# Soft attention kinds: GpSimd adds up the four whole key blocks, and one product with ones replaces four

## What is computed

```
x = x + attn_a(layernorm(x))   # "squared": scores squared instead of a softmax
x = x + ffn(layernorm(x))      # "gated": one key and value shared by the heads, picked by a top-1 gate; softmax
x = x + attn_b(layernorm(x))   # "mqa": one key and value shared by the heads; softmax; output projection
x = x + ffn(layernorm(x))      # "gated" again

# a soft kind, for one head:
att = softmax(where(causal, q @ k.T / sqrt(32), -inf))   # exp(scores - row maximum) / (sum of exp)
y   = att @ v
```

## Time and profile before

| | us |
|---|---|
| median of three runs | 4967.37 (4939.61 to 4968.83) |
| the profiled execution | 4950.15, of which the span 4948.4 |
| TensorE busy in the span | 4254.0 (86%) |
| VectorE busy | 1771.8 (36%) |
| ScalarE busy | 1551.4 (31%) |
| GpSimd busy | 850.5 (17%) |

### The profile page before, as it was taken

The page is one execution under the profiler, slowest core; times in us unless marked ns, Lnnn a source line. Parts: engine busy times, 40 slices in busy tenths (PEclk is TensorE's granted clock), DMA queues, the critical chain, the costliest instruction groups (busy, mean ns, idle before and its releaser), DMA issues.

```text
span 4948.4 us, 76270 instructions
## 1 busy us (share of the span) xinstructions
PE 4254.0 (86%) x32674; PEld 1835.6 (37%) x32674; DVE 1771.8 (36%) x2666; ACT 1551.4 (31%) x1985; POOL 850.5 (17%) x1495
## 2 busy tenths in 40 slices
PE   7899999969797887887888888888898987978886
PEld 4444434324333333333333333333333333333332
DVE  1222222224334433344343343433434344333342
ACT  1443343421323223233333333332223233232333
POOL 1212121110102102012021111212012012020011
PEclk9999999989999898999989999999999998999999
DMA  1001010030001001001010010101001001010010
GB/s 60 18 17 36 9 43 5 31 95 8 15 1 39 14 1 52 1 3 50 1 52 1 20 33 7 46 1 52 1 1 52 1 18 35 1 52 1 1 35 27
DMA packets 63404, 115.65 MB, mean 23 GB/s; under 512 B 8672, under 2 KB 9184, under 8 KB 63072
## 3 DMA queue, kind: packets, MB, share of 16 engines
q1 hardware_dynamic: 63072, 110.77, 6.9%
HBM read 77.19 MB, written 33.55 MB: 22 GB/s over the span
## 4 chain that ended last, share of the span: by engine, by line
PE 60%; DVE 6%; ACT 4%; issue 4%; POOL 2%; DMA 2%; SPq 0%; POOLq 0%; DVEq 0%
PE banks L1030 16%; PE banks L989 11%; PE banks L943 9%; PE banks L973 8%; PE banks L937 7%; DVE maxima_soft L771 5%; ACT probs_soft L692 4%; PE banks L970 3%; PE banks L998 2%; PE banks L1127 2%; DMA tiles_soft<-out 1%; POOL rest_soft L665 1%; POOL tiles_soft L597 1%; PE banks L1039 0%; PE banks L949 0%
## 5 line engine op out<-in xcount | busy, mean ns | idle before, releaser
L771 DVE TENSOR_REDUCE maxima_soft<-banks 128x2 f32<-128x1024 f32 (+3 forms) x1152 | 1036.5, 952 | 1507.3 <-PE banks L998 924.8
L692 ACT ACTIVATE probs_soft<-banks 128x1024 f32<-128x1024 f32 (+1 forms) x960 | 848.5, 936 | 1286.4 <-PE banks L973 1286.3
L989 PE MATMUL banks<-k_soft,q_soft 32*128 32x512 f32 (+3 forms) x4608 | 585.1, 578 | 215.9 <-ACT probs_soft L692 215.7
L606 POOL TENSOR_SCALAR_AFFINE_SELECT probs_soft<-probs_soft 128x512 f32<-128x512 f32 x384 | 239.2, 635 | 1841.5 <-ACT probs_soft L692 1839.2
L973 PE MATMUL banks<-q_soft,k_soft 32*128 32x512 f32 (+3 forms) x4608 | 487.2, 504 | 0.0
L1030 PE MATMUL banks<-probs_soft,v_soft 128*32 128x512 f32 (+3 forms) x4608 | 423.7, 510 | 2.0 <-POOL probs_soft L606 2.0
L1030 PE MATMUL banks<-probs_soft,ones 128*32 128x512 f32 (+3 forms) x4608 | 401.4, 489 | 0.0
L970 PE MATMUL banks<-shift_soft,ones 32*128 32x512 bf16 (+3 forms) x2304 | 201.2, 336 | 218.3 <-DVE maxima_soft L771 195.4
L989 PEld LDWEIGHTS banks<-k_soft,q_soft 32*128 32x128 f32 x4608 | 197.2, 194 | 463.5 <-issue 449.3
L692 ACT ACTIVATE probs_squared<-banks 128x1024 f32<-128x1024 f32 (+1 forms) x320 | 282.8, 936 | 239.8 <-PE banks L973 239.5
L1030 PEld LDWEIGHTS banks<-probs_soft,v_soft 128*32 128x32 f32 x4608 | 137.7, 113 | 278.6 <-issue 253.7
(11 more groups left out here) (151 smaller groups left out, 4206.8 us busy)
## 6 DMA issues: line engine op xcount, KB each, us to landing
tiles_soft<-out SPq DMA_DIRECT2D x96, 256.0 KB, 2.8
rest_soft<-out SPq DMA_DIRECT2D x96, 256.0 KB, 3.2
out<-rest_soft SPq DMA_DIRECT2D x96, 256.0 KB, 2.0
tiles_squared<-in_x SPq DMA_DIRECT2D x32, 256.0 KB, 2.9
rest_squared<-in_x SPq DMA_DIRECT2D x32, 256.0 KB, 3.2
out<-rest_squared SPq DMA_DIRECT2D x32, 256.0 KB, 2.0
raw_wq<-in_squared_wq SPq DMA_DIRECT2D x1, 1024.0 KB, 6.0
raw_wk<-in_squared_wk SPq DMA_DIRECT2D x1, 1024.0 KB, 8.2
```

The lines of the kernel that those rows point to most:

```text
L606: ins = pool.affine_select(out=cells, in_=cells, compare_op=ALU.is_ge, fill=0.0, base=0, pattern=[[0, HG], [1, P]], channel_multiplier=-1)
L692: act.activation(slot(ph, n)[:, 2 * a:2 * a + 2, 0:width], score_pair(e, a)[:, :, 0:width], ACT.Exp if soft else ACT.Square, scale=SCALE). ...
L771: ins = dve.reduce_max(m["maxima"][:, ph % 2, 2 * a:2 * a + 2, t, p], score_pair(e, a)[:, :, col:col + P * blocks], AX_X)
L989: ins = pe.matmul(psum[:, score_bank(e, i), col:col + P * blocks], m["q"][D * i:D * i + D, ph % NG, P * t:P * t + P], k_of(ph)[D * i:D * i ...
```

## The change

In soft kinds GpSimd adds the four slots of part B to one tensor full_sum (128 x 4 x 512 float32) in three instructions: at burst 4 slot 3 plus slot 4, at burst 5 that plus slot 5, at burst 6 that plus slot 6. Each waits for both exps of its burst and for the add before it. sm B then is 4 products with full_sum in place of 16, and waits for the third add. sm B moves from half 16 to half 17 in both acts, so behind rows(8) and mxr in the second. To make room in SBUF, logit_parts and v_parts become one buffer, side_parts. Weights of the planner stay.

```diff
+FULL = [n for n, burst in enumerate(KEY_BURSTS) if burst[1] == "B"]
...
         at[h].append(("av", of, part))
-        at[h + 1].append(("sm", of, part))
+        at[h + 2 if part == "B" else h + 1].append(("sm", of, part))
...
+        m["full_sum"] = sb("full_sum", [P, HG, CHUNK])
-        m["logit_parts"] = sb("logit_parts", [P, NC, CHUNK])
-        m["v_parts"] = sb("v_parts", [P, NC, CHUNK])
+        m["logit_parts"] = m["v_parts"] = sb("side_parts", [P, NC, CHUNK])
...
+                    elif soft and n > FULL[0]:
+                        pool.wait_ge(sg.probs_ready, 2 * (of_kind[e] + 1))
+                        added = (len(FULL) - 1) * ph + n - FULL[0] - 1
+                        if n == FULL[1] and ph:
+                            wait_work(pool, ("sm", ph - 1, part))
+                        elif n > FULL[1]:
+                            pool.wait_ge(sg.probs_added, added)
+                        before = slot(ph, FULL[0])[:] if n == FULL[1] else m["full_sum"][:]
+                        pool.tensor_tensor(m["full_sum"][:], before, slot(ph, n)[:], ALU.add).then_inc(sg.probs_added, 1)
...
+                    if u == "sm" and soft and part == "B":
+                        pe.wait_ge(sg.probs_added, (len(FULL) - 1) * (ph + 1))
+                        for i in range(HG):
+                            ins = pe.matmul(out[D * i:D * i + D, :], k["ones"][:], m["full_sum"][:, i, :], start=True, stop=True)
+                        products = []
```

More of the change, by code:

```diff
@@ L258, in __init__ @@
         self.probs_masked = sem("probs_masked")
+        self.probs_added = sem("probs_added")
         self.rows_scored = sem("rows_scored")
```

## The result

The changed kernel takes 4809.2 us in the median (4795.75 to 4812.38, 4 runs) against 4953.49 us before: ratio 0.9705, 95% interval 0.9658 to 0.9753. 88 us less were forecast, 144 came. The profiled execution took 4811.47 us with a span of 4809.8, against 4950.15 and 4948.4 before: 138.6 us less of span.

A forecast was written before the change was run, and what follows sets the result against it. The prediction took TensorE's list of work, with short holes, as the bound. Removal and holes gave 120.0 us; minus 14 (stage starts) and 18 (clock) left 88 us gained, so 4870 us was predicted, range 4830 to 4925.

The forecast's parts named there:

- What is removed, 131.0 us: TensorE at sm B: 3 of 4 product sets go, 2.73 us in each of 48 phases, 131.0 us saved.
- The holes, 25.2 + 7.4 us opened and 28.2 us closed: Around rows(8): moving sm B opens waits in front, 25.2 and 7.4 us, and fills those before keys(9), 28.2 us won.
- One assumption under it: In the 16 phases with fillers, the planner was expected to put the filler in front of rows(8); 6.2 us lost.
- The adds: On GpSimd: 144 adds of 4.47 us, 643 us more, beside other work, costing nothing below 8.7 us an add.
- The stage starts, 14 us: Phases 4, 8, 36 and 40: residual adds behind the third add end 3.5 us later, delaying loads; 14 us lost.
- the statement that in the other stages the stats stand far behind the adds: Other stages: outs and stats stand 11 us of PE work or more behind the add, or loads come behind burst 9.
- The clock, -18 us: Second act: the thin stretch grows, so the clock falls once more in one of four phases, 12 x 1.5 = 18 us lost.
- My bounds for it (0 to 73 us lost): Extra clock falls: from no more often (0) to once more in each of the 48 phases (73 us).
- In the first act nothing.: First act: the order of bursts and sm B doesn't change and its products stay, so no time change.
- The rival that had nothing lost: Clock falls as often as before and four stage starts absorb the delay: 120 to 131 us gained, 4830 to 4840; chance 0.13.

The follow-up runs named there:

- e9: Changed kernel with each GpSimd add one burst later, but sm B's 16 products from the slots kept and the adds' result unused; ratio 0.986 to the kernel before.
- e1: Kernel before with sm B, all 16 products, moved from half 16 to half 17, no adds; the planner rearranged other work; 4873.0 us, ratio 0.9863.
- e3: Changed kernel with sm B's 16 products from the slots kept, adds made and waited for but their result unused; 4900.95 us, ratio 0.9922 to the kernel before.
- e0: The changed kernel itself, measured again beside later runs on the same chip; 4808.23 us, ratio 0.9728 to the kernel before.
- e5: Changed kernel with each GpSimd add one burst later in GpSimd's order; 4787.83 us, ratio 0.9688 to the kernel before.
- e2: Changed kernel with sm B left at half 16, in front of rows(8), adds and 4 products kept; ratio 0.988 to the kernel before.
- e8: Kernel before with 4 products in place of 16, sm B at half 16, no adds, sum leaving out three blocks; ratio 0.985.
- e12: Kernel before, sm B still 16 products at half 16, plus four sets of idle products (16 products) behind rows(8); ratio 1.0214.
- e13: Kernel before with 4 products at half 16, no adds, three blocks left out, plus one idle set behind rows(8); ratio 0.9809.
- e11: Changed kernel with adds one burst later, plus 216 idle sets of 4 products of 384 columns between adjoining keys and rows bursts; 4745.18 us, ratio 0.9585.

## Why the prediction was right or wrong

It was wrong: the time, 4809.2 us, lies below the range of 4830 to 4925, and the gain is 1.6 times the forecast. The step that failed is the clock, which was to cost 18 us and gave a gain. Step by step:

- **What is removed, 131.0 us: nearly.** The group of products with ones went from 277.0 to 102.3 us, and the new line has 51.1 us: 123.6 us. A set that stands alone takes 1.07 us with its tail, not 0.91.
- **The holes, 25.2 + 7.4 us opened and 28.2 us closed: right.** PE's wait for exp grew by 35.3 us (215.7 to 251.0), that for maxima shrank by 22.0 (195.4 to 173.4; forecast 28.2 - 6.2 = 22.0). One assumption under it held only in part: of the 16 phases with fillers the filler went in front of rows(8) in 10; in phases 16, 20, 24, 28, 30 and 34 the planner left no filler beside rows(8) at all. That both sums come out so near is partly luck.
- **The adds: right in size and in place.** 4.51 us against 4.47, and PE waited for an add in one of 48 phases, 1.8 us. e9 shows that 144 of them beside this TensorE work cost nothing that could be measured (0.986, against 0.9863 in e1 without adds). What they would have cost on VectorE no run shows. VectorE's 576 large reductions took 1.221 us each, before 1.220: nothing.
- **The stage starts, 14 us: right for the four phases, but two more were hit.** e1 to e3, where only the adds differ, shows 14.1 us more of waiting in phases 4, 8, 36 and 40. Phases 21 and 25 add 8.9 us: the statement that in the other stages the stats stand far behind the adds went by the old plan, and the move changed the plan. The adds ahead of outputs and stats cost 20 (e0 to e5) to 28 us (e1 to e3), of which 17 and 24 are these waits. What else there is may be the clock (401 us at half clock in e0, 363 in e5), but that isn't shown. Against the kernel before the waits grew by only 9 us (135.4 to 144.2), since the move shortened them: 117.3 in e1. ln(0) in phase 4 waited 3.35 us longer, 3.5 forecast, but all such waits of that phase together stayed at 11 us.
- **The clock, -18 us: the step that failed, in its sign.** The rows showed a thin stretch (PE busy 7.11 of 12.8 us at 1.00) ahead of one at 0.51, and I reckoned the stretch by its length only: it got longer, so the clock had to get worse. My bounds for it (0 to 73 us lost) left no room for a gain. It got better, from 487 to 406 us at half clock, which by the estimate above is worth up to half of 81 us; the matmuls that stayed took 32.8 us less. e1 shows that this comes with the move and not by chance (0.962 to 0.966 against 0.948 to 0.954); e2 and e8 show that the change without the move would have gone as I feared and worse (0.988 and 0.985). I had treated the move as a matter of two holes, 28.2 - 32.6 us, that is a loss of 4; measured alone it is a gain of 68 us. How much of it is sm B's new place and how much the other work that the planner moved with it stays open; e12 and e13, which leave that work alone, show that dense work in the new place raises the clock by itself (0.961 to 0.962 against 0.950 to 0.954, and 0.951 to 0.954 against 0.932 to 0.944 in e8).
- **"In the first act nothing."** It was 9.5 us shorter in the profiled execution (GpSimd's first instruction of the second act at 1086.86, before at 1096.37). Most of it is the spread of single executions: the first exp of a soft phase comes at 1194.3 to 1203.9 us in the six traces with the old plan (mean 1199) and at 1190.0 to 1198.7 in eight with the changed one (mean 1194). Here too the planner moved some other work around sm B, so the order wasn't the same.

With the terms as measured: 123.6 - 13.3 (two waits) - 8.8 (ln) + up to 40.5 (clock) = up to 142.0 us, against 138.6 of span. The rival that had nothing lost (4830 to 4840) had the right side, but not the mechanism: it had the clock unchanged, and its times were still too high.

## What to carry to other kernels

When TensorE is the bound and its trace shows the granted clock below 1, a piece of work can have two values: what it takes, and what it does to the clock of what follows. Before a dense block is shortened or moved, lay the granted clock over the phases of the schedule (here by burst) and see in which bursts the slow time lies; then test the move alone and the removal alone: here the move changed the mean clock by +0.012, and the removal in the old place by -0.011. Look also at what a planner moves along with the piece. And where an in-order queue of an idle engine gets new work, it isn't its sum alone that matters but what stands behind it: 650 us of adds cost 20 to 28 us, and one place later gave 20 back.

## What the runs showed of the hardware that I had not expected

- The clock can fall where TensorE has only short holes. The kernel before in phase 5 (columns as in the stretches above), with no hole above 1.30 us: TensorE was busy 2.37 of 4.5 us at a clock of 1.00, and then had 0.56 for 7.8 us. But such holes don't always bring it: in e1 the whole stretch with the same work had 1.00, and so had the changed kernel with 12.51 busy of 18.50 us and holes up to 1.27 us. What decides between them no run shows.

```profile
1678.20:1682.70 4.50, 2.37 (x32) 1.10 (x32) 2.54 (x3) 1.53 (x3) 0.40 (x2) 1.00 0.00 0
1682.70:1690.50 7.80, 5.79 (x40) 2.48 (x35) 1.36 (x3) 2.68 (x4) 2.08 (x6) 0.56 0.00 0
```

- Work that nobody reads can make a kernel faster: 216 idle sets of four 384-column products in holes of PE took 38 us off the span and 104 us off the time at half clock in the second act (261 to 157).
- The mean clock of a kernel comes back to about 0.005 either way over runs and chips (the kernel before 0.946 to 0.956, e8 0.932 to 0.944), and the profiled executions differ from 0.937 (e2) to 0.973 (e11) between orders of nearly the same work. Here it can be read as a property of the schedule.
